# Four-corner blend with at most one SBUF input per vector operation

## The reference

```python
y0 = jnp.floor(py)
x0 = jnp.floor(px)
wy = (py - y0)[:, None]
wx = (px - x0)[:, None]
return v00 * (1 - wy) * (1 - wx) + v01 * (1 - wy) * wx + v10 * wy * (1 - wx) + v11 * wy * wx
...
sampled = bilinear_sample(x, py, px) * mask[:, None]
return jnp.einsum('bckhw,ock->bohw', sampled, reg_w.reshape(O, C, k * k))
```

## Time and profile before

| | us |
|---|---|
| median of 3 runs | 7705.86 (7702.70 to 7709.04) |
| the profiled execution | 7708.3 |
| its span, first to last instruction | 7706.6 |
| POOL busy in the span | 5167.0 |
| PE busy | 5235.2 |
| DVE busy | 4707.9 |
| ACT busy | 2571.4 |

### The profile page before, as it was taken

One profiled execution on the slowest core, in us unless ns is written; L12 is line 12 of the kernel. 1 busy time (PEld: TensorE's weight loads), 2 busy tenths in 40 slices (PEclk: granted clock), 3 DMA queues, 4 the chain that ended last, 5 costly groups with the idle time before them and its releaser, 6 DMA issues. The chain is left out here.

```text
span 7706.6 us, 69512 instructions
## 1 busy us (share of the span) xinstructions
PE 5235.2 (68%) x19428; PEld 3288.9 (43%) x19428; DVE 4707.9 (61%) x5704; ACT 2571.4 (33%) x6392; POOL 5167.0 (67%) x4363
## 2 busy tenths in 40 slices
PE   3666666666666666666666655656565665899998
PEld 3444444444444444444444322222222222677777
DVE  2666666666666666666666656565556534566665
ACT  0332333332323232323232322222223243366664
POOL 1888888888888888888888888888888820122221
PEclk9888888888888888898888767676776687899999
DMA  6666666666666666666666656565656565555555
GB/s 200 178 203 189 196 187 198 195 193 175 200 174 192 177 192 175 190 177 194 176 189 176 181 163 179 164 178 163 180 164 176 163 215 192 185 150 149 147 153 174
DMA packets 718752, 1387.41 MB, mean 180 GB/s; under 512 B 235528, under 2 KB 401288, under 8 KB 716816
## 3 DMA queue, kind: packets, MB, share of 16 engines
q0 software_dynamic: 327680, 1044.66, 47.8%
q1 hardware_dynamic: 362464, 320.40, 13.6%
q10 hardware_dynamic: 28336, 19.10, 0.8%
HBM read 1268.08 MB, written 115.72 MB: 180 GB/s over the span
## 5 line engine op out<-in xcount | busy, mean ns | idle before, releaser
L447 POOL DMA_INDIRECT G<-table,om x3840 | 4897.3, 1275 | 1246.2 <-issue 950.9
L588 DVE SCALAR_TENSOR_TENSOR G<-G,omw 128x1536 f32<-128x1536 f32 x960 | 1687.6, 1758 | 1959.3 <-DMA G<-table,om 1937.9
L482 ACT ACTIVATE G<-G,om 128x128 f32<-128x128 f32 x3840 | 1227.3, 390 | 4208.5 <-DMA G<-table,om 4171.6
L700 PE MATMUL ps_y<-sT,R 128*128 128x512 f32 x3840 | 2474.0, 781 | 106.5 <-ACT sT L490 103.8
L688 PE MATMUL ps_t<-ident,acc 128*128 128x128 f32 x3840 | 767.2, 333 | 2071.6 <-DVE acc L598 2033.6
L688 PEld LDWEIGHTS ps_t<-ident,acc 128*128 128x128 f32 x3840 | 499.4, 165 | 2639.0 <-DVE acc L598 2556.7
L594 DVE SCALAR_TENSOR_TENSOR G<-G 128x1024 f32<-128x1024 f32 x960 | 1176.4, 1225 | 106.1 <-ACT G L482 3.6
L700 PEld LDWEIGHTS ps_y<-sT,R 128*128 128x128 f32 x3840 | 865.8, 249 | 818.1 <-issue 691.8
L676 PEld LDWEIGHTS ps_o<-wom,win 128*128 128x128 f32 x6272 | 968.5, 203 | 403.9 <-issue 403.4
L676 PE MATMUL ps_o<-wom,win 128*128 128x147 f32 (+1 forms) x6272 | 974.9, 305 | 56.1 <-DMA win<-xn 31.1
L1489 DVE TENSOR_TENSOR vl<-ps_v,vh 128x512 fp32r<-128x512 f32 x1024 | 657.2, 686 | 334.1 <-ACT vh L1438 334.0
(11 more groups left out here) (171 smaller groups left out, 1622.7 us busy)
## 6 DMA issues: line engine op xcount, KB each, us to landing
tt<-kern_dram SPq DMA_DIRECT2D x512, 192.0 KB, 3.4
G<-table,om POOLq DMA_INDIRECT x3840
win<-xn SPq DMA_DIRECT2D x154, 224.0 KB
y_dram<-yb SPq DMA_DIRECT2D x64, 512.0 KB
yin<-y_dram SPq DMA_DIRECT2D x16, 2048.0 KB, 8.8
ut<-spec_dram POOLq DMA_DIRECT2D x256, 96.0 KB, 3.3
spec_dram<-spec_hi SPq DMA_DIRECT2D x64, 256.0 KB, 2.6
ut<-spec_dram POOLq DMA_DIRECT2D x256, 48.0 KB, 3.0
```

The costliest lines, as they stand in the source:

```text
L447: pool.indirect_dma_start(G[k % RING][:, j, :], None, tables[g // GI], bass.IndirectOffsetOnAxis(ap=om[g % 2][:, j, 0, k:k + 1].bitcast(I3 ...
L482: last = nc.scalar.activation(G[k % RING][:, j, 0:C], G[k % RING][:, j, 0:C], ACT.Copy, scale=om[g % 2][:, j, 1, k:k + 1])
L588: nc.vector.scalar_tensor_tensor(part(1, 4), part(1, 4), 1.0, omw[g % 2][:, :, k:k + 1].to_broadcast([128, 12, C]) .rearrange("p (j c) d - ...
L700: last = nc.tensor.matmul(ps_y[:, half, :], R[:, k, 128 * half:128 * half + 128], sT[n % 2][:, :], start=(k == t0), stop=(k == ends[br] - 1))
```

## The change

The blend is written so that no DVE operation has more than one input in SBUF.

- The corner weights of 30 taps (half a group) are copied from `omw` to a PSUM tile `ps_w` by a new DVE operation `spread`, once in 30 steps, and the multiplication of line 588 reads its weights there. It becomes a tensor_tensor, still 1536 columns.
- ACT writes the scaled first corner to a PSUM tile `ps_a` instead of back to G. `ps_a` is single, so `corner0(n)` now waits until `blended` has counted step n - 1.
- Lines 594 and 598 (1024 and 512 columns) are replaced by three additions of 512 columns: corner 1 plus `ps_a` into `ps_a`, corner 2 plus `ps_a` into `ps_a`, corner 3 plus `ps_a` into `acc`. Each waits for the one before (`added`).
- PSUM has eight banks, so the two `ps_t` become one. `turn(n)` waits for `copied` of step n - 1 instead of n - 2, and ACT's `copy_out` runs one step behind instead of two.
- An own block at the end of the stage clears six semaphores.

```diff
-        ps_t = [ctx.enter_context(nc.psum_tensor(f"ps_t{h}", [C, CH], F32)) for h in range(2)]
+        ps_t = ctx.enter_context(nc.psum_tensor("ps_t", [C, CH], F32))
+        ps_a = ctx.enter_context(nc.psum_tensor("ps_a", [128, 4, C], F32))
+        ps_w = ctx.enter_context(nc.psum_tensor("ps_w", [128, 4 * 3, HALF_TAPS], F32))
...
                 act.wait_ge(gathered[k % RING], (n // RING) * 64 + 64)
+                act.wait_ge(blended, n + RING)
                 for j in range(4):
-                    last = nc.scalar.activation(G[k % RING][:, j, 0:C], G[k % RING][:, j, 0:C], ACT.Copy,
+                    last = nc.scalar.activation(ps_a[:, j, :], G[k % RING][:, j, 0:C], ACT.Copy,
                                                 scale=om[g % 2][:, j, 1, k:k + 1])
...
-                if LAG <= n < NT + LAG:
-                    copy_out(n - LAG)
+                if 1 <= n <= NT:
+                    copy_out(n - 1)
...
+            def spread(n):
+                g, k = divmod(n, TAPS)
+                if g:
+                    dve.wait_ge(om_loaded[g % 2], 32 * ((g + 1) // 2))
+                else:
+                    dve.wait_ge(offsets_ready, 4)
+                nc.vector.tensor_copy(ps_w[:, :, :], omw[g % 2][:, :, k:k + HALF_TAPS]).then_inc(weights_spread, 1)
...
                 dve.wait_ge(gathered[k % RING], (n // RING) * 64 + 64)
-                nc.vector.scalar_tensor_tensor(part(1, 4), part(1, 4), 1.0,
-                                               omw[g % 2][:, :, k:k + 1].to_broadcast([128, 12, C])
-                                               .rearrange("p (j c) d -> p j c d", j=4),
-                                               ALU.mult, ALU.mult).then_inc(weighted, 1)
+                dve.wait_ge(weights_spread, n // HALF_TAPS + 1)
+                nc.vector.tensor_tensor(three, three, ps_w[:, :, h:h + 1].to_broadcast([128, 12, C])
+                                        .rearrange("p (j c) d -> p j c d", j=4), ALU.mult).then_inc(weighted, 1)
                 dve.wait_ge(first_corner, n + 1)
                 dve.wait_ge(weighted, n + 1)
-                nc.vector.scalar_tensor_tensor(part(0, 2), part(2, 4), 1.0, part(0, 2), ALU.mult, ALU.add)\
-                    .then_inc(paired, 1)
+                nc.vector.tensor_tensor(ps_a[:, :, :], corner(1), ps_a[:, :, :], ALU.add).then_inc(added, 1)
+                if h == HALF_TAPS - 1 and n + 1 < NT:
+                    spread(n + 1)
+                dve.wait_ge(added, 2 * n + 1)
+                nc.vector.tensor_tensor(ps_a[:, :, :], corner(2), ps_a[:, :, :], ALU.add).then_inc(added, 1)
                 dve.wait_ge(turned, n + 1)
-                dve.wait_ge(paired, n + 1)
-                nc.vector.scalar_tensor_tensor(acc[n % 3][:, :, :], whole(1), 1.0, whole(0), ALU.mult, ALU.add)\
-                    .then_inc(blended, 1)
+                dve.wait_ge(added, 2 * n + 2)
+                nc.vector.tensor_tensor(acc[n % 3][:, :, :], corner(3), ps_a[:, :, :], ALU.add).then_inc(blended, 1)
...
                 pe.wait_ge(blended, n + 1 + RING)
-                if n >= 2:
-                    pe.wait_ge(copied, n - 1)
+                if n >= 1:
+                    pe.wait_ge(copied, n)
...
+        work.close()
+        with nc.Block() as clearing:
+            @clearing.sync
+            def _(sp):
+                for s in [xn_turned, xn_copied, xn_summed, xn_stored, table_written, ln_step]:
+                    sp.sem_clear(s)
```

More of the change, by code:

```diff
@@ L18 @@
 RR = 10
+HALF_TAPS = 30
 NG = B * GI
@@ L277, in stage_branches @@
         weighted = sem("weighted")
-        paired = sem("paired")
+        weights_spread = sem("weights_spread")
+        added = sem("corners_added")
         blended = sem("blended")
@@ L306, in stage_branches @@
         LAG = 2
+        assert TAPS == 2 * HALF_TAPS
         X_FIRST, X_STEP = 14, 28
-        block = ctx.enter_context(nc.Block())
+        work = ExitStack()
+        block = work.enter_context(nc.Block())
         ends = [t0 + n for t0, n in BRANCHES]
@@ L489, in copy_out @@
                     act.wait_ge(summed, n - 1)
-                nc.scalar.activation(sT[n % 2][:, :], ps_t[n % 2][:, :], ACT.Copy).then_inc(copied, 1)
+                nc.scalar.activation(sT[n % 2][:, :], ps_t[:, :], ACT.Copy).then_inc(copied, 1)
             def evacuate(g, br):
@@ L581, in weights @@
                 dve.sem_inc(offsets_ready, 1)
+            def spread(n):
[5 more added lines that the diff above has]
+                nc.vector.tensor_copy(ps_w[:, :, :], omw[g % 2][:, :, k:k + HALF_TAPS]).then_inc(weights_spread, 1)
             def blend(n):
                 g, k = divmod(n, TAPS)
-                part = lambda lo, hi: G[k % RING][:, :, lo * C:hi * C].rearrange("p j (c d) -> p j c d", c=hi - lo)
@@ L586, in blend @@
-                whole = lambda c: G[k % RING][:, :, c * C:(c + 1) * C]
+                corner = lambda c: G[k % RING][:, :, c * C:(c + 1) * C]
+                three = G[k % RING][:, :, C:4 * C].rearrange("p j (c d) -> p j c d", c=3)
+                h = k % HALF_TAPS
                 dve.wait_ge(gathered[k % RING], (n // RING) * 64 + 64)
-                nc.vector.scalar_tensor_tensor(part(1, 4), part(1, 4), 1.0,
-                                               omw[g % 2][:, :, k:k + 1].to_broadcast([128, 12, C])
-                                               .rearrange("p (j c) d -> p j c d", j=4),
-                                               ALU.mult, ALU.mult).then_inc(weighted, 1)
+                dve.wait_ge(weights_spread, n // HALF_TAPS + 1)
@@ L633, in _ @@
                 weights(m)
+            spread(0)
             for n in range(NT + 5):
@@ L684, in turn @@
                 pe.wait_ge(blended, n + 1 + RING)
-                if n >= 2:
-                    pe.wait_ge(copied, n - 1)
+                if n >= 1:
+                    pe.wait_ge(copied, n)
                 for j in range(4):
-                    last = nc.tensor.transpose(ps_t[n % 2][:, 128 * j:128 * j + 128], acc[n % 3][:, j, :], ident[:, :])
+                    last = nc.tensor.transpose(ps_t[:, 128 * j:128 * j + 128], acc[n % 3][:, j, :], ident[:, :])
                 last.then_inc(turned, 1)
```

## The result

The changed kernel took 7838.08 us, the median of 4 runs (7821.15 to 7843.78), against 7704.28 for the kernel before in the same comparison: a ratio of 1.0172, 95% interval 1.0153 to 1.0191. It is 1.7% slower. The forecast was 6444 us, the range ended at 6880, and slower had a chance of 0.08.

The account below looks back on a forecast made before the run. POOL's own gather issue rate was taken to bound the kernel. 7706.6 - 1268 (held time) + 1 (clearing block) + 5 (stalls) = 6445 us of span, 6446 profiled, less 2.4 for the median: 6444 us, range 6430 to 6880.

Parts of the forecast that it names:

- held gathers: POOL's gathers that wait for DVE operations with two SBUF inputs; freeing them was to save 1268 us.
- Only if every other engine gets through a step in 4.98 us: Condition for getting the whole saving: DVE, ACT, PE and DMA must each keep up with POOL's 4.98 us step.
- the ring covers that: With one `ps_t`, PE can be hardly more than a step late; POOL's six gather buffers absorb it.
- ACT's work costs nothing: `corner0`, at most 1.56 us a step, hides under the multiplication's 1.757 us; cost nothing.
- the DMA share of 0.83: Transfers need 4.15 us of all 16 engines per 4.98 us step, so they were called no bound.
- Lags do no harm: POOL may run up to six steps ahead, some 25 us, while DVE's longest side-work burst is a few us.
- 4.60, 4.53 and 4.19 us of work a step: DVE's predicted need per step in three stretches, blend plus side work, below POOL's 4.98 us.
- The fixed PSUM excess: Skill's rule of some 0.065 us more per PSUM source on DVE, 0.26 us a step; the forecast did not adopt it.
- The rule on SBUF inputs: DVE operations with at most one SBUF input do not hold POOL's gathers, which then take 0.945 us.
- B: Rival: multiplication and additions both slow with PSUM operands, 2.1 us a step more on DVE, 7943 us; chance 0.05.
- C: Rival: gathers are still held by the long multiplication despite PSUM, 7706 to 7800 us; chance 0.06.
- A: Rival: DVE or PE becomes the bound, still faster than before, 6935 or 7040 us; chance 0.17.

Follow-up runs that it names:

- E12: Changed kernel plus 26-column POOL memsets, one behind each of three gathers of a step and two behind the fourth: 7380.83 us, ratio 0.9593.
- E9: Changed kernel plus 40-column POOL memsets, one behind each of three gathers of a step and two behind the fourth: 7433.90 us, ratio 0.9661.
- E10: Changed kernel plus 60-column POOL memsets, one behind each of three gathers of a step and two behind the fourth: 7497.34 us, ratio 0.9744.
- E4: Changed kernel with gathers of 512 bytes a row instead of 2048, three corners left out: 7771.12 us.
- E3: Kernel before with each two-input operation of the blend replaced by bn_stats with one SBUF input, the blend's result left out: 7795.61 us.
- E7: Changed kernel plus 8-column POOL memsets, one behind the first and third gather of a step, two behind the second and fourth: 7493.76 us.
- E5: Changed kernel plus three chained 8-column POOL memsets behind every fourth gather: 7348.98 us, ratio 0.9553.
- E1: Changed kernel with the multiplication reading its weights from SBUF again: 7641.36 us.

## Why the prediction was wrong

**What bounds the kernel, and the held gathers (-1268 us): right, and incomplete.** POOL's pace did bound the kernel, and the gathers came down from 4897.3 us to 3641.2, 1256 less. Between E12, E9 and E10 time follows the pace. By the one-for-one slope a pace of 1.25 us would give 7433.90 - 0.244 x 3840 = 6497 us (an estimate, far outside the paces that it was read from), 53 above the forecast. The arithmetic of the sum wasn't the failure.

**"Only if every other engine gets through a step in 4.98 us": this is where it failed, in the steps on PE, ACT and DMA.** Three sentences fell together: that PE is late by hardly more than a step since "the ring covers that", that ACT's work costs nothing, and that the DMA share of 0.83 is "No bound. Unheld gathers already run at the new spacing of 1.25 us". All three add up what engines *execute*, and each was right in that: PE, ACT and DVE had no more work than forecast, and the transfers weren't slower (E4). What no term stood for is the time from the end of a PE instruction to the arrival of its increment, taken as constant and so put at nothing in the sum. It was 0.01 us in the median before, with 7 increments over 1 us; at the new spacing 606 of 1495 took over 1 us, and up to 12.9: 2356.6 us in 278 waits ahead of line 497, and 1179 us in gaps with all three engines idle. "Lags do no harm" fell with it: the ring lets POOL run six steps ahead of DVE, but here DVE, ACT and PE stood still together, and by the prediction's own 4.60, 4.53 and 4.19 us of work a step DVE could have made up only some 520 us in the 960 steps (an estimate from the earlier trace rows). The trace of before held the new spacing mostly for three gathers in a row, between two held ones, and never for more than seven; it was no evidence for 3840 of them. It also held a trace of the effect, 7 late increments of up to 5.1 us, which I hadn't looked for.

**DVE: right.** 1748 ns with a broadcast from PSUM, 697 and 695 with PSUM read and written by one operation; busy time in all 4806.7 us against 4707.9. The fixed PSUM excess that the Trainium skill gives in "VectorE: DVE Perf Modes", the section on the TRN2 errata, doesn't show here either: 697, 695 and 687 ns beside the 692 of the SBUF form. **The rule on SBUF inputs: right.** Beside an operation with one SBUF input gathers take 943 ns at the least and 949 in the median, as "SBUF — State Buffer", "Who interferes with whom", of the Trainium skill would have it; E3's bn_stats give 946.

**PE's single `ps_t` and the shorter lag: not the cause.** E3 has both tiles and LAG 2 and is as late. And where the increments are on time, the single tile costs next to nothing: in E10 PE waited 19.5 us in 18 waits for ACT's copy. They may set how soon a late increment stops the others, which I haven't measured apart: E3 was 42.5 us faster than the kernel after, but its DVE work differs too.

**The rivals.** "Slower" had B and a part of C behind it. B was wrong in its mechanism: its 7943 us is near the 7838 by chance, and its sign (multiplication at 2.8 us) isn't there. A and C aren't there either. The sign named for A, POOL waiting for `blended` and DVE for `first_corner`, did appear, without the longer additions that were to come with it. A rival was missing: that something other than the engines' busy time keeps the hand-offs on time, and that the removed stalls provide it.

**What stays open.** What in the chip delays the increments. The ends of matmuls are modelled in the profile, so it can't be told whether the increments alone were held or the matmuls too; both fit what is recorded. Of the 412 increments that came over 3 us late in the kernel after, 123 arrived while a gather was running and 186 came 2.2 to 3.4 us after the end of the last one. Why ACT's and DVE's are never late isn't explained. Whether the limit near 1.48 us moves with PE's own load wasn't tried. And one rival stands untested: every run on record has the profiler's span and clock, none is known to have run without a trace, and dense gathers also cost the trace many of its semaphore records (E7, at 1.508 us, has 85% of DVE's and 81% of ACT's again). So it isn't shown that the increments would be late with no trace being taken.

## What to carry to other kernels

A stall that paces an engine may protect others: before removing it, look in the trace for how long the new pace has ever been held, and price the hand-offs, not only the busy times. When a dense stream of indirect gathers makes engines wait for "remote", compare the moment a semaphore rises with the end of the instruction that sets it; a few cheap operations between gathers turned a loss of 1.7% into a gain of 4.5% (E5) here. Sweep the pace: 1.398 us gave 7536, 1.435 gave 7349, 1.510 gave 7497, so the best one that was tried still has hundreds of late increments and lies beside a steep rise.

## What the runs showed of the hardware

- Indirect gathers issued by POOL closer than some 1.48 us in mean go with late semaphore increments of TensorE in these traces: none over 1 us at 1.51, 4 of up to 2.3 us at 1.494, 24 of up to 4.4 us at 1.479, hundreds of up to 20 us at 1.25 to 1.435. The mean is one of a few steps: before and in E1, 1.59 and 1.56 over the stage, 7 and 30 came late behind dense stretches. Bytes (1045 or 290 MB) and rows (128 or 64) make no difference; PE's transposes never began more than 0.45 us after the last of DVE's, ACT's and PE's work ahead of them in any run, so the increments of DVE and ACT that they wait for were on time.
- A gather that starts under a DVE operation with two SBUF inputs ends 0.82 us past the end of it; before, three such operations a step gave a pace of 1.59 us; in E1 one of them gave 1.56.
- A gather of 64 rows costs POOL 906 ns and one of 128 rows 948, so halving its rows saves 42 ns.
